# Layer 1's k placed by transfers inside SBUF, and layer 1's normalisation moved from ScalarE to GpSimd

## The chip, the cores and the metric

One Trainium2 chip, one core of it. The metric is the device time of one execution in microseconds (us); the kernel before was run three times: 1116.78, 1117.99 and 1119.48 us, median 1117.99 us.

## What is computed

The input is 8 sequences of 512 tokens with 128 channels. There are two layers. In each, the input is normalised over its channels, and the sum of an attention-like part and a feed-forward part is added to it.

```python
xn = _layernorm(x)                       # layer 0
x = x + _L0_attn_ref(xn, ...) + _L0_ffn_ref(xn, ...)   # state-space scan; one of 8 experts per token
xn = _layernorm(x)                       # layer 1
x = x + _L1_attn_ref(xn, ...) + _L1_ffn_ref(xn, ...)   # windowed attention; gated feed-forward

# inside _L1_attn_ref
q = _split_heads(x @ Wq + bq)            # 16 heads of 8 channels
k = _split_heads(x @ Wk + bk)
v = _split_heads(x @ Wv + bv)
scores = jnp.einsum('bhqd,bhkd->bhqk', q, k) / math.sqrt(HEAD_DIM)
scores = scores + _sliding_window_mask(s, WINDOW_SIZE)   # 32 positions to either side
```

## The kernel before, in words

**Stages.** The work is a pipeline over the 8 sequences, written out by hand. A turn is one pass of `iterations` (line 460); it has 28 slots, and `plan()` (line 80) lists what is done in each slot. In turn `it`, four lanes run side by side: "pre" prepares the scan of sequence it+1 (projections, convolution, gates), "scan" does the 16 steps of the scan of sequence it, "attn" does layer 1 of sequence it-1, and "late" and "finish" end layer 1 of sequence it-2. Each engine walks through the same list of units in the same order and does its own part of each, so every engine is a queue in order, and only semaphores tie the queues together. The experts of layer 0 run beside the first turns.

**The scan.** In each step n, ScalarE makes the decays (`decays`, line 911: two exponentials, dA), VectorE multiplies the input by a broadcast row into PSUM (`times_b`, line 725: dBu), VectorE scans (line 733: hst), and hst times another broadcast row gives hc, on GpSimd (line 1100), or on VectorE in steps 2, 3 and 15 (lines 743, 749). TensorE sums hc into y_bank (`sum_y`, line 1189). The broadcast rows come by the SP queue (`bc_rows`, line 530) into a ring of 4 buffers, bcr; after step k's unit "spread" the rows of step k+3 are sent for, and that waits until hc of step k-1 is done.

**Layer 1's front, slots 0 to 6 of a turn.** Slot 1: x1r (line 831). Slot 2, unit ln_a: VectorE's statistics (lines 837 to 844), then GpSimd's power and product (lines 1124, 1126: rstd1, shift1). Slot 3: step 2 of the scan, then ln_b: ScalarE normalises four blocks of 128x128 into xn1 (line 968), TensorE transposes each (line 1250), ScalarE copies the bank to xn1T (line 971). The pre lane's conv1 (VectorE, line 761) and the matmul of zg0 (line 1202) stand behind it. Slot 4: q and k (TensorE line 1254), ScalarE writes q in four copies, each with its own scale, into qbd (line 976), and k into kT (line 985): kT has four row blocks, heads 4r to 4r+3 of k lie in partitions 32r to 32r+31 of block r, and the rest of kT is zero. In the same slot stand the pre lane's tanh (line 935, with a load of the function table ahead of it) and sg0 (VectorE line 772), which needs that tanh. Slot 5: step 3 of the scan, v0 and v1 (TensorE 1261, ScalarE 990), conv2, and the tanh for sg1. Slot 6: v2, v3, conv3, sg1. Slot 7: step 4 of the scan. The first scores, which read kT, stand in slot 10 (line 1273).

**What sets the order around the change.** On ScalarE: the decays of step 3, then xn1, the copy to xn1T, the table load, the tanh for sg0, four qbd, four kT, the decays of step 4, v0, v1, the tanh for sg1. On VectorE: scan 2, dBu 3, hc 2, conv1 (two instructions), sg0, scan 3, dBu 4, hc 3, four of conv, sg1, scan 4. On TensorE: sum_y of step 1, the four transposes, zg0, q, k. On GpSimd: hc 0 and hc 1 (slots 0, 1), line 1124 and line 1126, then nothing of the scan before hc 4 in slot 7; line 1114 (the product of the finish lane) stands in slot 5. On the SP queue: in slot 0 the 16 + 4 + 1 transfers of `own_heads` (line 535), then the rows of steps 4 and 5, then in slot 5 those of step 6, in slot 7 of step 7.

**Buffers.** rbuf (line 266) holds the routing's logits in the first turn and zeros for one transfer; after that it is unused.

Of the kernel before, what the change touches and what calls it, by code (L numbers as in the profile page):

```python
# [11 lines left out]
ALU = mybir.AluOpType  # L12
# [182 lines left out]
def program(nc, hidden, pack, wx_d, ffn_d, xn_d, xs_d, ys_d, bc_d, rd_d, out):  # L195
    ctx = ExitStack()
    with ctx:
# [134 lines left out]
        xgT = [p_flat[:, 3 * L + k * P:3 * L + (k + 1) * P] for k in range(MOE_BANKS)]  # L332
        h_T = [fh[:, k, :] for k in range(MOE_BANKS)]
        o_own = fth
        rd_rows = y_out[:].rearrange("p j d -> p (j d)")
        ys = [y_out[:], fsg[:].rearrange("p (j d) -> p j d", d=H)]

# [42 lines left out]
        s_slot = sem("slots_of_sequence")  # L380
        s_moe = sem("expert_rows_in")
        s_conv = sem("conv_steps")
        s_tap = sem("first_tap_ready")
        s_tg = sem("gate_tanh_ready")
        s_xsq = sem("xsq_ready")
# [93 lines left out]
        @block.sync  # L479
        def _(sp):  # L480
            def x_load(k):
                sp.dma_start(xa[k % 4], seq(hidden, k)).then_inc(s_xa[k % 4], 16)
            x_load(0)
            x_load(1)
            sp.dma_start(pk[:], pack).then_inc(s_pack, 16)
            x_load(2)
            x_load(3)
            sp.dma_start(ffn_i, ffn_d).then_inc(s_ffn, 16)

            def weights(m):  # L490
                e = sp.value_load(tile_e[0:1, m:m + 1], min_val=0, max_val=E - 1)
                sp.dma_start(wx[m % WX_RING], wx_d[:, bass.ds(e, 1), :].rearrange("p o c -> p (o c)")).then_inc(
                    s_wx[m % WX_RING], 16)

            def early(name, k):
                if name == "norm":
                    sp.wait_ge(s_axn, (k + 1) * NT)
                    sp.dma_start(seq(xn_d, k), xna[k]).then_inc(s_xast[k], 16)
                    if k + 4 < B:
                        x_load(k + 4)  # L500
                    if k == 0:
                        sp.wait_ge(s_xast[0], 16)
                        sp.dma_start(x_in[:], seq(xn_d, 0)).then_inc(s_xin, 16)
                elif name == "scatter":
                    sp.wait_ge(s_route, ROUTE_TILES)
                    for m in range(3):
                        weights(m)
                elif name == "gather":
                    sp.wait_ge(s_scat, 16 * TT)
                    for k in range(B):  # L510
                        sp.wait_ge(s_xast[k], 16)
                    for r in range(2):
                        sp.dma_start(xg[r], tiles(xs_d, r)).then_inc(s_xg[r], 16)
                    for m in range(3, WX_RING):
                        weights(m)
                elif name == "xt":
                    r = k // MG
                    if k % MG == MG - 1 and r + 2 < NM // MG:
                        sp.wait_ge(s_xgT, k + 1)
                        sp.dma_start(xg[r % 2], tiles(xs_d, r + 2)).then_inc(s_xg[r % 2], 16)  # L520
                elif name == "add":
                    r = k // MG
                    if k + WX_RING < NM or k % MG == MG - 1:
                        sp.wait_ge(s_myc, k + 1)
                    if k + WX_RING < NM:
                        weights(k + WX_RING)
                    if k % MG == MG - 1:
                        sp.dma_start(tiles(ys_d, r), ys[r % 2]).then_inc(s_yst[r % 2], 16)

            def bc_rows(b, n):  # L530
                before(sp, s_hc, b * N + n - RING + 1)
                rows = bc_d[b:b + 1].rearrange("o (k n) t -> o n k t", k=2)
                sp.dma_start(bcr[n % RING][:], rows[:, n, :, :].to_broadcast([P, 2, L])).then_inc(s_bcr[n % RING], 16)

            def own_heads(b):
                done1(sp, b, f"gate{HC - 1}")
                done1(sp, b, "oL")
                for r in range(RG):
                    for h in range(4):
                        q = slice(32 * r + HD * h, 32 * r + HD * h + HD)  # L540
                        sp.dma_start(o_own[q, :], o_all[q, h, :, :].rearrange("p g q -> p (g q)")).then_inc(s_own, 16)
                done1(sp, b, "rdT")
                for r in range(RG):
                    rows = rd_d[b, r] if isinstance(b, int) else rd_d[bass.ds(b, 1), r].rearrange("o h g q -> (o h) g q")
                    sp.dma_start(rows.rearrange("h g q -> g h q"), rdenT[r * G:(r + 1) * G, :, :]).then_inc(s_rdst, 16)
                sp.wait_ge(s_rdst, b * 64 + 64)
                before(sp, s_out, b * 16)
                rows = rd_d[b:b + 1] if isinstance(b, int) else rd_d[bass.ds(b, 1)]
                sp.dma_start(rd_rows, rows.rearrange("o r h g q -> (o r h) (g q)").unsqueeze(1).to_broadcast(
                    [RG * 4, HD, L])).then_inc(s_rdin, 16)  # L550

            def body(it, par):
                for name, k, b, odd in units(it):
                    early(name, k)
                    if name == "dtT":
                        done0(sp, b, "dtT")
                        sp.dma_start(bc_d[b], dtT[R:XW, :]).then_inc(s_bcd, 16)
                    if name == "start":
                        sp.wait_ge(s_bcd, b * 16 + 16)
                        for n in range(RING - 1):  # L560
                            bc_rows(b, n)
                    if name == "spread" and k + RING - 1 < N:
                        bc_rows(b, k + RING - 1)
                    if name == "spread" and k == 0 and b >= 2:
                        own_heads(b - 2)
                    if name == "xnT" and (not isinstance(b, int) or b + 1 < B):
                        full0(sp, b, "xnT")
                        sp.wait_ge(s_xast[b + 1], 16)
                        sp.dma_start(x_in[:], seq(xn_d, b + 1)).then_inc(s_xin, 16)
                    if name == "rdT":  # L570
                        if b >= B - 2:
                            own_heads(b)
                    if name == "y_out":
                        done1(sp, b, "fin")
                        sp.dma_start(seq(out, b), y_out[:]).then_inc(s_out, 16)
                    if name == "rows":
                        done1(sp, b - 1, "out")
                        sp.dma_start(x_res[:], seq(hidden, b)).then_inc(s_xres, 16)
            for name, k in LEAD:
                early(name, k)  # L580
            for it in range(-1, B + 2):
                body(it, it % 2)
            sp.wait_ge(s_out, 16 * B)
# [302 lines left out]
        def _(act):  # L886
# [76 lines left out]

            def layer1(name, k, b, par):
                if name == "ln_b":
                    act.wait_ge(s_rstd1, b * 2 + 2)
                    for j in range(NT):
                        s.activation(xn1[:, j, :], x1r[par][:, j, :], ACT.Identity, bias=shift1[:, j:j + 1],
                                     scale=rstd1[:, j:j + 1]).then_inc(s_xn1, 1)
                    full1(act, b, "xnT")  # L970
                    s.copy(xn1T[:, WIN:WIN + L], w1k("xnT")[:]).then_inc(free1("xnT"), 1)
                elif name == "q":
# [5 lines left out]
                    last.then_inc(free1(name), 1)  # L978
                elif name == "k":
                    full1(act, b, name)  # L980
                    if isinstance(b, int) and b == 0:
                        act.wait_ge(s_clear, 1)
                    for r in range(RG):
                        q = slice(32 * r, 32 * r + 32)
                        last = s.activation(kT[q, r, WIN:WIN + L], w1k(name)[q, :], ACT.Identity, bias=pc("bk")[q, :])
                    last.then_inc(free1(name), 1)
                elif name in ("v0", "v1", "v2", "v3"):
                    j = int(name[1:])
                    full1(act, b, name)
# [54 lines left out]
        def _(pool):  # L1044
# [58 lines left out]
            def body(it, par):  # L1103
                for name, k, b, odd in units(it):
# [14 lines left out]
                    elif name == "bc":  # L1119
                        bc(b)  # L1120
                    elif name == "ln_a":
                        pool.wait_ge(s_stat1, b * 10 + 10)
                        before(pool, s_xn1, b * NT)
                        g_.tensor_tensor(rstd1[:], var1[:], minus_half[:, 0:NT], ALU.pow).then_inc(s_rstd1, 1)
                        pool.wait_ge(s_rstd1, b * 2 + 1)
                        g_.tensor_tensor(shift1[:], shift1[:], rstd1[:], ALU.mult).then_inc(s_rstd1, 1)
            iterations(pool, body)


        @block.tensor  # L1130
        def _(pe):
# [100 lines left out]
            def layer1(name, k, b, par):  # L1232
# [31 lines left out]
                elif name == "scores":  # L1264
                    key = f"s{k}"
                    if k == 0:
                        done1(pe, b, "q")
                        done1(pe, b, "k")
                    take1(pe, b, key)
                    v = 0 if k == 0 else (2 if k == G - 1 else 1)  # L1270
                    t.matmul(w1k(key)[:, 0:RG * KW], identb[:], bandb[:, v, :, :].rearrange("p r k -> p (r k)"),
# [118 lines left out]
```

## Time and profile before

| what | value |
|---|---|
| runs | 1116.78, 1117.99, 1119.48 us; median 1117.99 |
| profiled execution, its own time | 1115.84 us |
| its span | 1114.1 us |
| granted TensorE clock, mean | 0.925 of full speed |
| TensorE matmul busy | 861.4 us, 77% |
| VectorE busy | 810.0 us, 73% |
| ScalarE busy | 679.8 us, 61% |
| GpSimd busy | 386.2 us, 35% |

The span runs from the first to the last instruction of the program; the execution's own time has 1.7 us more around it. Busy shares are means over the whole span. The times of the rows below are microseconds from the start of this span.

### The profile page before, as it was taken

The page shows a single profiled execution, that of the slowest core. Times are in us where ns is not written, and L with a number is a line of the kernel's source. Part 1 is how long each engine was busy: PE and PEld are TensorE (multiplying, and loading weights), DVE is VectorE, ACT ScalarE, POOL GpSimd, SP SyncE. Part 2 cuts the span into 40 slices and gives each one's busy share as a digit, 9 for nine tenths or more (in the row PEclk, how much of TensorE's full clock was granted, in tenths as well). Part 3 has the DMA queues.
Part 4 walks back from the last instruction along what each step waited for, and adds up shares of the span by engine and source line. Part 5 has one row for each costly group of instructions (what it writes and reads, how often), then busy time and mean ns, then how long its engine had stood idle before and what let it go on. Part 6 is the DMA issues. An engine that isn't in the chain of part 4 may idle for free.

```text
span 1114.1 us, 13822 instructions
## 1 busy us (share of the span) xinstructions
PE 861.4 (77%) x4346; PEld 477.5 (43%) x4346; DVE 810.0 (73%) x1010; ACT 679.8 (61%) x2045; POOL 386.2 (35%) x228
## 2 busy tenths in 40 slices
PE   3553879886697779777977797788878886897893
PEld 2412667663343444334434443343335333443532
DVE  7764444677978897889788968897889788974120
ACT  2132556665577657766776667666756684685680
POOL 3175122213632263226322632254225422641000
PEclk9556999998999999999998989999989899999995
DMA  8164779963331433244324332443234333430001
GB/s 295 39 212 120 228 230 287 264 192 76 82 97 58 123 86 97 57 119 91 97 59 115 93 85 70 105 102 89 71 93 102 80 77 105 102 88 11 19 1 30
DMA packets 85304, 121.14 MB, mean 109 GB/s; under 512 B 8560, under 2 KB 43760, under 8 KB 85104
## 3 DMA queue, kind: packets, MB, share of 16 engines
q1 hardware_dynamic: 78944, 113.45, 36.6%
q0 software_dynamic: 6288, 6.82, 2.7%
q8 instruction: 35, 0.57, 0.2%
q14 instruction: 37, 0.30, 0.1%
HBM read 105.82 MB, written 12.32 MB: 106 GB/s over the span
## 4 chain that ended last, share of the span: by engine, by line
PE 37%; DVE 26%; issue 11%; POOL 11%; ACT 10%; DMA 3%; SPq 1%; DVEq 0%; POOLq 0%; ACTq 0%
PE y_bank L1189 11%; DVE hst L733 10%; POOL hc L1100 4%; PE more L1287 4%; DVE dBu L725 4%; POOL xs_d L1068 3%; POOL x_res L1084 3%; PE work_l L1273 2%; PE work L1273 2%; ACT qbd L976 2%; PE work L1202 2%; ACT dA L917 2%; DVE dc L810 2%; DVE nmax L847 1%; DMA hst<-in_hidden 1%
## 5 line engine op out<-in xcount | busy, mean ns | idle before, releaser
L1100 POOL TENSOR_TENSOR hc<-hst,bcr 128x1024 f32<-128x1024 f32 x102 | 244.3, 2395 | 530.6 <-DVE dBu L725 488.0
L1189 PE MATMUL y_bank<-hc,pk 128*128 128x512 f32 x512 | 269.8, 653 | 83.1 <-POOL hc L1100 66.0
L733 DVE TENSOR_TENSOR_SCAN hst<-dA,dBu 128x1024 f32<-128x1024 f32 x128 | 291.5, 2278 | 3.4 <-issue 2.9
L725 DVE TENSOR_TENSOR dBu<-dtu,bcr 128x1024 f32<-128x1024 f32 x128 | 175.7, 1373 | 12.9 <-DVE hst L733 0.5
L917 ACT ACTIVATE dA<-dt,neg_a 128x511 f32<-128x511 f32 x256 | 171.6, 726 | 17.7 <-DVE hst L733 14.4
L1189 PEld LDWEIGHTS y_bank<-hc,pk 128*128 128x128 f32 x512 | 94.7, 201 | 186.2 <-POOL hc L1100 81.5
L1011 ACT COPY pT<-more 96x512 f32<-96x512 f32 x128 | 74.4, 581 | 100.0 <-PE more L1287 98.3
L1287 PE MATMUL more<-pk,pexp 128*96 128x128 f32 x512 | 102.6, 291 | 10.9 <-ACT pexp L1001 10.4
L1287 PEld LDWEIGHTS more<-pk,pexp 128*96 128x96 f32 x512 | 61.3, 128 | 84.7 <-issue 58.6
L1001 ACT ACTIVATE pexp<-work,nmax 128x96 f32<-128x96 f32 x256 | 83.2, 338 | 15.9 <-DVE nmax L847 15.8
L1001 ACT ACTIVATE pexp<-work_l,nmax 128x96 f32<-128x96 f32 x256 | 83.1, 338 | 1.2 <-DVE nmax L847 1.2
L847 DVE TENSOR_REDUCE nmax<-work 128x4 f32<-128x384 f32 x64 | 35.4, 553 | 51.2 <-PE work L1228 47.7
L1084 POOL DMA_INDIRECT x_res<-ys_d,slot_b x32 | 51.2, 1601 | 9.0 <-issue 9.0
L1273 PE MATMUL work_l<-kT,qbd 128*128 128x384 f32 x128 | 53.2, 498 | 0.0
L1001 ACT ACTIVATION_READ_ACCUMULATOR pexp<-work_l,nmax 128x1 f32 x256 | 52.2, 204 | 0.0
L1001 ACT ACTIVATION_READ_ACCUMULATOR pexp<-work,nmax 128x1 f32 x256 | 51.9, 203 | 0.0
L1273 PE MATMUL work<-kT,qbd 128*128 128x384 f32 x128 | 51.7, 486 | 0.0
L847 DVE TENSOR_REDUCE nmax<-work_l 128x4 f32<-128x384 f32 x64 | 35.4, 553 | 21.7 <-PE work_l L1228 21.1
L1202 PE MATMUL work<-xnT,pk 128*128 128x512 f32 x64 | 38.6, 688 | 14.4 <-ACT hs L930 9.4
L1114 POOL TENSOR_TENSOR fth<-fth,y_out 128x512 f32<-128x512 f32 x8 | 11.6, 1445 | 109.5 <-DMA y_out<-rd_d 109.5
L928 ACT ACTIVATE z<-work,half_c 128x512 f32<-128x512 f32 x16 | 12.4, 777 | 51.5 <-PE work L1202 44.8
L864 DVE TENSOR_TENSOR y_out<-x1r,work 128x512 f32<-128x512 f32 x8 | 5.5, 682 | 40.8 <-PE work L1316 40.8
(303 smaller groups left out, 1475.7 us busy)
## 6 DMA issues: line engine op xcount, KB each, us to landing
bcr<-bc_d SPq DMA_DIRECT2D x128, 512.0 KB
qbd<-in_wx SPq DMA_DIRECT2D x8, 578.0 KB, 4.2
o_all<-in_wx SPq DMA_DIRECT2D x8, 578.0 KB
pT<-in_wx SPq DMA_DIRECT2D x8, 578.0 KB
kT<-in_wx SPq DMA_DIRECT2D x8, 578.0 KB, 5.1
vw<-in_wx SPq DMA_DIRECT2D x8, 578.0 KB, 5.2
xs_d<-rbuf POOLq DMA_DIRECT2D x1, 2560.0 KB, 9.8
hst<-in_hidden SPq DMA_DIRECT2D x8, 256.0 KB, 4.9
```

The source lines that it names most:

```text
L725: v.tensor_tensor(dBu[:], dtu[par], bcr[n % RING][:, 0:1, :].to_broadcast([P, NH, L]), ALU.mult).then_inc(s_dBu, 1)
L733: v.tensor_tensor_scan(hst[n % 2][:].rearrange("p h t -> p (h t)"), dA[n % 2][:].rearrange("p h t -> p (h t)"), dBu[:].rearrange("p h t -> ...
L847: v.tensor_reduce(nmax[:, k, :], w1k(f"s{k}")[:, 0:RG * KW].rearrange("p (r k) -> p r k", r=RG), AX_X, ALU.max, negate=True).then_inc(s_nm ...
L917: s.activation(dA[n % 2][:, h, 1:L], dt[par][:, h, 1:L], ACT.Exp, scale=neg_a[:, h, n:n + 1]).then_inc(s_dA, 1)
L1001: last = s.activation(pexp[k % 2][:, r, :], w1k(f"s{k}")[:, r * KW:(r + 1) * KW], ACT.Exp, bias=nmax[:, k, r:r + 1], accum_out=den[:, r, k ...
L1011: s.copy(pT[k % 4][:], w1k(f"pT{k}")[0:KW, :]).then_inc(free1(f"pT{k}"), 1)
L1084: g_.indirect_dma_start(x_res[:, j, :], None, ys_d.rearrange("i j p d -> (i j p) d"), bass.IndirectOffsetOnAxis(ap=slot_b[:, j:j + 1], axi ...
L1100: g_.tensor_tensor(hc[n % 2][:], hst[n % 2][:], bcr[n % RING][:, 1:2, :].to_broadcast([P, NH, L]), ALU.mult).then_inc(s_hc, 1)
L1189: last = t.matmul(y_bank[h][:], ident, hc[n % 2][:, h, :], start=False, stop=(n == N - 1))
L1202: t.matmul(bank0[:], pc("in_proj")[:, k * P:(k + 1) * P], xnT[:], start=True, stop=True).then_inc(s_full0, 1)
L1273: last = t.matmul(w1k(key)[:, 0:RG * KW], qbd[:, k, :, :].rearrange("p h q -> p (h q)"), kT[:, :, k * GQ:k * GQ + KW], start=False, stop=True)
L1287: last = t.transpose(w1k(key)[0:KW, r * P:(r + 1) * P], pexp[k % 2][:, r, :], ident)
```

## The change

ScalarE no longer normalises xn1: GpSimd does it, with four tensor_scalar instructions (times rstd1, plus shift1) behind its own power and product in slot 2. ScalarE writes k once, as one 128x512 tile with its bias, into the free half of rbuf (k_flat_b); the SP queue waits for that in slot 4, and then issues four transfers, each of 32 partitions x 512 f32, from k_flat_b into the four row blocks of kT. TensorE's first scores wait for these transfers (semaphore s_kin) in place of ScalarE's write. ScalarE's next write of k waits for the transfers of the sequence before.

```diff
+        k_flat_b = rbuf[:, 1, :]
...
+        s_kin = sem("k_blocks_in")
...
 (SP queue, body)
+                    if name == "k":
+                        if b == 0:
+                            sp.wait_ge(s_clear, 1)
+                        done1(sp, b, "k")
+                        for r in range(RG):
+                            q = slice(32 * r, 32 * r + 32)
+                            sp.dma_start(kT[q, r, WIN:WIN + L], k_flat_b[q, :]).then_inc(s_kin, 16)
...
 (ScalarE, layer1)
                 if name == "ln_b":
-                    act.wait_ge(s_rstd1, b * 2 + 2)
-                    for j in range(NT):
-                        s.activation(xn1[:, j, :], x1r[par][:, j, :], ACT.Identity, bias=shift1[:, j:j + 1],
-                                     scale=rstd1[:, j:j + 1]).then_inc(s_xn1, 1)
                     full1(act, b, "xnT")
                     s.copy(xn1T[:, WIN:WIN + L], w1k("xnT")[:]).then_inc(free1("xnT"), 1)
...
                 elif name == "k":
                     full1(act, b, name)
-                    if isinstance(b, int) and b == 0:
-                        act.wait_ge(s_clear, 1)
-                    for r in range(RG):
-                        q = slice(32 * r, 32 * r + 32)
-                        last = s.activation(kT[q, r, WIN:WIN + L], w1k(name)[q, :], ACT.Identity, bias=pc("bk")[q, :])
-                    last.then_inc(free1(name), 1)
+                    before(act, s_kin, b * 64)
+                    s.activation(k_flat_b, w1k(name)[:], ACT.Identity, bias=pc("bk")).then_inc(free1(name), 1)
...
 (GpSimd, ln_a)
                         g_.tensor_tensor(shift1[:], shift1[:], rstd1[:], ALU.mult).then_inc(s_rstd1, 1)
+                        pool.wait_ge(s_rstd1, b * 2 + 2)
+                        for j in range(NT):
+                            g_.tensor_scalar(xn1[:, j, :], x1r[(par + odd) % 2][:, j, :], rstd1[:, j:j + 1], shift1[:, j:j + 1],
+                                             ALU.mult, ALU.add).then_inc(s_xn1, 1)
...
 (TensorE, scores, k == 0)
-                        done1(pe, b, "k")
+                        pe.wait_ge(s_kin, b * 64 + 64)
```

## Rows read from the trace of the kernel before

**Rows 1.** The page: the chain that ended last, shares of the span by engine.

```profile
PE 37%; DVE 26%; issue 11%; POOL 11%; ACT 10%; DMA 3%; SPq 1%; DVEq 0%; POOLq 0%; ACTq 0%
```

**Rows 2.** Waits: who waited for whom; total us, times, longest.

```profile
DVE sg L772 <- ACT tg L935: 17.4, 11, 3.9
```

**Rows 3.** Timeline, turn from 478 us: start, us, engine, line, operation, [idle before].

```profile
485.43 0.20 POOL L1126 TENSOR_TENSOR shift<-shift,rstd 128x4 f32<-128x4 f32 x1
485.68 1.88 PE L1189 MATMUL y_bank<-hc,pk 128*128 128x512 f32 x4
486.53 1.23 DVE L725 TENSOR_TENSOR dBu<-dtu,bcr 128x1024 f32<-128x1024 f32 x1
488.26 1.64 ACT L968 ACTIVATE xn<-x1r,shift,rstd 128x128 f32<-128x128 f32 x4
488.81 1.41 DVE L761 SCALAR_TENSOR_TENSOR z<-hs,half_c,z 128x512 f32<-128x512 f32 x2
488.89 1.39 PE L1250 MATMUL work_l<-pk,xn 128*128 128x128 f32 x4 [1.33 <-ACT xn L968]
489.06 9.52 SPq L533 DMA_DIRECT2D bcr<-bc_d  x4
490.32 0.58 ACT L971 COPY xn1T<-work_l 128x512 f32<-128x512 f32 x1 [0.42 <-PE work_l L1250]
492.84 0.69 DVE L772 SCALAR_TENSOR_TENSOR sg<-tg,work 128x512 f32<-128x512 f32 x1 [2.62 <-ACT tg L935]
495.35 2.74 ACT L985 ACTIVATE kT<-work_l,pk 32x512 f32<-32x512 f32 x4
501.07 0.69 DVE L772 SCALAR_TENSOR_TENSOR sg<-tg,work 128x512 f32<-128x512 f32 x1 [0.23 <-ACT tg L935]
508.18 1.23 DVE L725 TENSOR_TENSOR dBu<-dtu,bcr 128x1024 f32<-128x1024 f32 x1
```

**Rows 4.** The same view, turns from 588 us (sg0, sg1) and 814 us (sg0).

```profile
604.46 0.69 DVE L772 SCALAR_TENSOR_TENSOR sg<-tg,work 128x512 f32<-128x512 f32 x1 [3.94 <-ACT tg L935]
...
613.12 0.69 DVE L772 SCALAR_TENSOR_TENSOR sg<-tg,work 128x512 f32<-128x512 f32 x1 [0.66 <-ACT tg L935]
...
829.75 0.69 DVE L772 SCALAR_TENSOR_TENSOR sg<-tg,work 128x512 f32<-128x512 f32 x1 [2.93 <-ACT tg L935]
```

**Rows 5.** The same view: the turns from 925 us and 1018 us, and the first.

```profile
936.23 1.65 ACT L968 ACTIVATE xn<-x1r,shift,rstd 128x128 f32<-128x128 f32 x4 [3.93 <-POOL shift L1126]
...
947.01 2.29 DVE L733 TENSOR_TENSOR_SCAN hst<-dA,dBu 128x1024 f32<-128x1024 f32 x1 [2.90 <-issue]
...
1035.74 1.11 PE L1261 MATMUL work_l<-pk,xn1T 128*96 128x128 f32 x8 [1.50 <-ACT kT L985]
...
270.05 0.68 DVE L772 SCALAR_TENSOR_TENSOR sg<-tg,work 128x512 f32<-128x512 f32 x1
```

**Rows 6.** Groups of GpSimd by line and shape: busy us, mean ns.

```profile
L1124 POOL TENSOR_TENSOR rstd<-var,minus_half 128x4 f32<-128x4 f32 x8 | 8.3, 1039 | 14.3 <-DVE shift L844 14.3
```

**Rows 7.** Timeline at 526 us and 938 us: GpSimd and VectorE side by side.

```profile
526.08 2.93 POOL L1100 TENSOR_TENSOR hc<-hst,bcr 128x1024 f32<-128x1024 f32 x1
526.76 4.17 DVE L725 TENSOR_TENSOR dBu<-dtu,bcr 128x1024 f32<-128x1024 f32 x1
528.39 1.45 POOL L1093 TENSOR_TENSOR xdn<-xdr,pk 128x384 f32<-128x384 f32 x1
531.01 2.35 POOL L1100 TENSOR_TENSOR hc<-hst,bcr 128x1024 f32<-128x1024 f32 x1 [1.18 <-DVE dBu L725]
...
938.23 1.22 DVE L743 TENSOR_TENSOR hc<-hst,bcr 128x1024 f32<-128x1024 f32 x1
938.23 2.34 POOL L1114 TENSOR_TENSOR fth<-fth,y_out 128x512 f32<-128x512 f32 x1 [2.04 <-DMA y_out<-rd_d]
```

**Rows 8.** Timeline: the product on GpSimd at 491 us, and the SP queue's issues.

```profile
474.79 10.68 SPq L541 DMA_DIRECT2D fth<-o_all  x16
...
491.86 1.27 POOL L1114 TENSOR_TENSOR fth<-fth,y_out 128x512 f32<-128x512 f32 x1 [6.22 <-DMA y_out<-rd_d]
512.69 0.81 PE L1273 MATMUL work<-kT,qbd 128*128 128x384 f32 x2
```

## The prediction

> **What bounds the kernel now.** I read the chain that ended last, then the waits, then the timeline of each turn's first 25 us. The chain has no single owner: TensorE 37%, VectorE 26%, ScalarE 10%, GpSimd 11% [rows 1]. So a change is worth what it does at the wait that ends last where it is made, and the place is layer 1's front. There VectorE, which carries the scan, stands still for ScalarE: sg0 and sg1 wait for a tanh, 17.4 us in 11 waits [rows 2]. In the turn from 478 us sg0 waits 2.62 us and sg1 0.23 us [rows 3]. Three turns have this form (from 366, 478 and 703 us). Two have the form of 588 us, with 3.94 and 0.66 us [rows 4]; the other, from 814 us, has 2.93 [rows 4] and 0.67. ScalarE reaches that tanh late because it first does four xn1 blocks (488.26 to 489.90), waits for the transposes, copies at 490.32 and loads a table; sg0 starts 2.52 us after the copy starts [rows 3]. The last turn with a scan has no tanh, but VectorE waits 2.90 us before scan 4, whose decays stand behind kT on ScalarE [rows 5]. The turn after it has no scan: TensorE waits 1.50 us for the bank that kT is read from [rows 5]. In the first such turn sg0 does not wait [rows 5]; there VectorE itself is the bound.
>
> **xn1 leaves ScalarE.** ScalarE loses 1.64 us a turn [rows 3]. The gain is less, since the transposes become the limit: TensorE's sum_y ends at 485.68 + 1.88 = 487.56, the transposes start at 488.89 now [rows 3]. They can come 1.33 us earlier if GpSimd is in time, and copy, table load, tanh and sg0 come with them. I take 1.33 in all five turns with a wait at sg0; the other four repeat these rows.
>
> **xn1 on GpSimd.** No GpSimd tensor_scalar is in the trace. From below: its smallest product, 4 elements a partition, takes 0.20 us [rows 3]. From above: the power on 4 elements, 1.04 us [rows 6]. Nearest are the products: 2.35 us for 1024 elements [rows 7] and 1.27 for 512 [rows 8], so 2.11 ns an element and 0.19 us fixed, and 0.46 us for 128. I take 0.45 each, 1.8 us for four, from 485.63 (end of line 1126) to 487.43. The fourth transpose now starts at about 489.9 and would at 488.6: in time. GpSimd has nothing of the scan there before step 4. Behind the new work stands only line 1114, which starts at 491.86 [rows 8].
>
> The two engines hold each other up. At 526 us VectorE's dBu (1.23 us elsewhere) took 4.17 us, until two products of GpSimd had ended; at 938 us GpSimd's product took 2.34 instead of 1.27 us beside VectorE's hc [rows 7]. Whoever is in first keeps the other out. Here GpSimd is in at 485.63, while VectorE scans, and scans are not slowed in the trace; dBu 3 is due at 486.53 [rows 3]. It would wait until 487.43, 0.90 us. VectorE had 2.62 us to spare at sg0: its conv1 ends at 488.81 + 1.41 = 490.22, then at 491.12, and the tanh allows sg0 at 492.84 - 1.33 = 491.51. So the delay is covered, with 0.39 us left. In general, with t for one block, sg0 gains the smaller of 1.33 and W - (4t - 0.90), W being its wait: 3.52 - 4t for the three turns, 4.84 - 4t and 3.83 - 4t for the two.
>
> The Trainium skill (SBUF — State Buffer, "Who interferes with whom") says the same of the pair of ports, and that the first to issue holds it for one whole instruction. The trace agrees as far as the 4.17 us go, but there a second GpSimd instruction still kept VectorE out. Taken strictly, the rule lets VectorE in between two blocks; that is the second rival below.
>
> The Trainium skill (GPSIMD Engine Reference, "Engine selection") puts one-input work on GpSimd at roughly line rate, against about twice VectorE's time with two inputs. No run here shows it; an estimate by it is some 0.3 us a block, and the sum would be 1 us better.
>
> **k written once.** Four instructions take 2.74 us on ScalarE [rows 3]; one of the same length takes a quarter, so 2.05 us go. Where sg1 waits, only its wait is won, since VectorE's own eight us of work between sg0 and sg1 then bound: 0.23 in three turns, 0.66 and 0.67 in two. In the turn from 925 us the decays come 2.05 earlier, inside VectorE's 2.90. In the last, TensorE's 1.50.
>
> **The transfers.** Sixteen issues of this kind take 10.68 us on the SP queue [rows 8], so four take 2.7. k is written at about 494.5 (now 495.35 to 498.09, less 1.33 and 2.05, with the q copies unchanged), issued by 497.3, and read by the scores at 512.69 [rows 8], 511 then. I cost the landing at nothing: 13 us cover it; gone, it would cost its length once a turn. Behind SP's wait stand the scan rows of steps 6 and 7. Those of step 6 go out with the four from 489.06 now, at about 497.5 then; they are used at 508.18 [rows 3], 506.5 then. 9 us cover them. Step 7's wait for hc 3 anyway. The ring's slots, and rbuf, are free.
>
> **Where it doesn't help.** In the turns from 925 and 1018 us xn1 already waited for GpSimd [rows 5], so the move costs 4 x 0.45 - 1.65 = 0.15 each. In the first turn VectorE has nothing to spare and loses the 0.90. Later stages of a turn hang on VectorE's u and scans, so I let the gain pass through.
>
> **Sum:** 5 x 1.33 = 6.65; sg1 3 x 0.23 + 0.66 + 0.67 = 2.02; 2.05 - 0.15 = 1.9; 1.5 - 0.15 = 1.35; minus 0.9. That is 11.0 us. The profiled execution has 1115.84, so 1104.8; the median is 2.15 above it, so **1107**. At t = 0.20 it is 6.65 + 2.02 + 2.05 + 1.5 = 12.2, so 1105.8. At t = 1.04: 3 x (-0.64) + 0.68 - 0.33 + 2.02, then 2.05 - 2.51, 1.5 - 2.51 and -3.26, together -4.3, so 1122.3. It turns at about t = 0.93.
>
> **Rivals.**
> 1. *Only k pays.* The transposes come no earlier than now (GpSimd's blocks are slower beside VectorE, or t is about 0.8), but nothing is lost: 2.02 + 1.9 + 1.35 - 0.9 = 4.4 us, so 1113.6. For it: 2.34 instead of 1.27 us [rows 7].
> 2. *VectorE gets in between, slower than before.* dBu 3, hc 2 and conv1 follow one another, each with two SBUF inputs. If dBu 3 enters at 486.53 and GpSimd's last two blocks wait for all three, they end at 490.22 + 0.90 = 491.12, the copy starts 0.42 later at 491.54 instead of 490.32: 1.22 lost in three turns (-3.66), +0.10 and -0.91 in the two with longer waits, 2.02 from sg1, in the turn from 925 us (hc 2 ends 939.45 [rows 7], xn1 at 940.35 instead of 937.88) 2.05 - 2.47, then 1.35 without a scan, and 1.22 + 2.62 = 3.84 lost in the first. Together -5.4, so 1123.4. It decides from the moment that two blocks have to wait. Against it: at 526 us back-to-back GpSimd work was not interrupted [rows 7]. The page named above speaks for it.
> 3. *t near 1 us:* 1122, as worked out. Against it: the power is the dearest row.
> 4. *Nothing arrives at the end:* the stages after slot 10 hang on TensorE and GpSimd, which hold 48% of the chain [rows 1], and take the gain back: 1117 to 1118. Against it: their first work of the turn waits for VectorE.
>
> **Chances.** My forecast 0.60; rival 1, 0.14; rival 2, 0.11; rival 3, 0.05; rival 4, 0.10. Under 0.2% (2.2 us) a measurement of this kernel can't tell from no change; most of rival 4 falls there. Faster 0.76, same 0.08, slower 0.16. The likeliest case's own range is 1105 to 1110; the range 1102 to 1116 takes in rival 1, the scatter of the runs and some gain I haven't seen; it leaves out rivals 2 and 3 and most of 4.
>
> **What would show it.** GpSimd's line of xn1 at about 450 ns; dBu 3 at some 2.1 us; the wait at sg0 down to about 0.4 us and at sg1 gone; ScalarE's busy time down by 8 x (1.64 + 2.05) = 29.5 us; no wait on s_kin at the first scores; SP's rows of step 6 eight us later and no VectorE wait for them. Wrong if xn1 on GpSimd ends after 489 us in the turn of rows 3, if dBu 3 runs between blocks, or if a VectorE wait of like size shows up later in each turn.

## The result, and the profile after

The changed kernel takes 1121.45 us (median of 12 runs, 1119.51 to 1123.58), the kernel before 1118.16 (median of 12). The ratio is 1.0029, with a 95% interval of 1.0019 to 1.0039: slower by 0.3%, where the prediction had 1107 us and a range that ended at 1116. The profiled execution took 1120.89 us, its span 1119.0. Ratios here and below are estimates from the executions that were not disturbed, against those of the kernel before beside them, and not quotients of the medians; one of the 12 of experiment 1, with 1134.53 us at a granted clock of 0.814, is left out of its ratio.

The page of the changed kernel, busy times and the chain that ended last, to be read against [rows 1]:

```profile
PE 861.7 (77%) x4346; PEld 479.2 (43%) x4346; DVE 807.5 (72%) x1010; ACT 651.4 (58%) x1989; POOL 419.7 (38%) x260
PE 35%; DVE 29%; POOL 13%; issue 12%; ACT 4%; DMA 4%; SPq 1%; DVEq 0%; POOLq 0%; ACTq 0%
```

ScalarE has lost 28.4 us of work, and its share of the chain went from 10% to 4%. What it left, GpSimd and VectorE took up. GpSimd's new line, and the wait at sg0, which stood in [rows 2]:

```profile
L1130 POOL TENSOR_SCALAR xn<-x1r,rstd,shift x32: 447/452/2517, 266.7 to 1033.4; 128x128 f32<-128x128 f32 x32
DVE sg L781 <- ACT tg L944: 19.4, 7, 3.3
```

Of the 32 blocks the shortest took 447 ns, the median 452, the longest 2517. The length of a block alone is what the prediction took, 0.45 us. But the wait at sg0 and sg1 is 19.4 us in 7 waits, and was 17.4 in 11. The timeline of one turn shows why (this is the turn of [rows 3]; start, us, engine, line; the blocks one by one):

```profile
489.01 2.27 DVE L742 TENSOR_TENSOR_SCAN hst<-dA,dBu 128x1024 f32<-128x1024 f32 x1
490.60 0.45 POOL L1130 TENSOR_SCALAR xn<-x1r,rstd,shift 128x128 f32<-128x128 f32 x1
491.04 0.45 POOL L1130 TENSOR_SCALAR xn<-x1r,rstd,shift 128x128 f32<-128x128 f32 x1
491.38 1.23 DVE L734 TENSOR_TENSOR dBu<-dtu,bcr 128x1024 f32<-128x1024 f32 x1
491.47 2.52 POOL L1130 TENSOR_SCALAR xn<-x1r,rstd,shift 128x128 f32<-128x128 f32 x1
492.53 1.22 DVE L752 TENSOR_TENSOR hc<-hst,bcr 128x1024 f32<-128x1024 f32 x1
493.66 1.53 DVE L770 SCALAR_TENSOR_TENSOR z<-hs,half_c,z 128x512 f32<-128x512 f32 x2
493.97 1.38 POOL L1130 TENSOR_SCALAR xn<-x1r,rstd,shift 128x128 f32<-128x128 f32 x1
495.77 0.59 ACT L976 COPY xn1T<-work_l 128x512 f32<-128x512 f32 x1 [2.56 <-PE work_l L1255]
498.30 0.69 DVE L781 SCALAR_TENSOR_TENSOR sg<-tg,work 128x512 f32<-128x512 f32 x1 [3.11 <-ACT tg L944]
506.82 2.28 DVE L742 TENSOR_TENSOR_SCAN hst<-dA,dBu 128x1024 f32<-128x1024 f32 x1
```

The first two blocks run under scan 2 and take 0.45 us each. VectorE's dBu starts at 491.38, nine hundredths before the third block, and keeps its 1.23 us. The third block takes 2.52: it ends at 493.99, 0.24 us after hc, so it waited for dBu and hc. It was let in ahead of conv1, whose first instruction takes 0.11 us more than its second:

```profile
493.66 0.86 DVE L770 SCALAR_TENSOR_TENSOR z<-hs,half_c,z 128x512 f32<-128x512 f32 x1
494.44 0.75 DVE L770 SCALAR_TENSOR_TENSOR z<-hs,half_c,z 128x512 f32<-128x512 f32 x1
```

The fourth takes 1.38 and ends at 495.35, 0.16 us after the second of these and 0.83 after the first: it waited for both. The four blocks have these lengths, within 0.02 us, in all of turns 1 to 6. Turn 7 has no convolution; VectorE goes from hc to scan 3, and there the fourth block takes 0.45 beside it:

```profile
943.52 2.28 DVE L742 TENSOR_TENSOR_SCAN hst<-dA,dBu 128x1024 f32<-128x1024 f32 x1
943.83 0.45 POOL L1130 TENSOR_SCALAR xn<-x1r,rstd,shift 128x128 f32<-128x128 f32 x1
```

So dBu, hc and conv1, which read two tiles of SBUF each, shut a block out, and the scan, which takes its dBu from PSUM, does not: the first two blocks and turn 7's fourth run beside one. In turns 1 to 6 the four blocks take 4.75 us in place of 1.8. In this turn ScalarE stands idle for 2.56 us before its copy, and VectorE waits 3.11 us at sg0 for what it has itself held up.

The same in numbers for every turn: from the start of scan 2 to the start of scan 4 (line 733 before, 742 after), each the difference of two starts in the traces.

| turn | before | changed | k part alone | xn1 part alone | both, VectorE held |
|---|---|---|---|---|---|
| 1 | 14.59 | 17.77 | 14.49 | 19.32 | 15.48 |
| 2 | 17.53 | 17.81 | 17.20 | 18.13 | 15.48 |
| 3 | 17.52 | 17.81 | 17.21 | 19.00 | 16.67 |
| 4 | 19.28 | 17.81 | 17.20 | 18.99 | 16.03 |
| 5 | 17.51 | 17.96 | 18.76 | 19.00 | 15.47 |
| 6 | 19.29 | 17.81 | 17.21 | 18.99 | 16.54 |
| 7 | 12.30 | 13.31 | 10.12 | 15.50 | 11.37 |

Turns 2, 3 and 5 are the three of the prediction, 4 and 6 the two with a longer wait, 7 the last with a scan. Changed less before: +3.2 in turn 1, +0.3, +0.3 and +0.45 in the three, -1.5 twice, +1.0 in turn 7, together 2.3 us. One scan later, turn 7 has lost 1.4 more (18.64 us from scan 2 to scan 5 in place of 16.19). After the last copy to xn1T (1027.47 before, 1034.46 changed), in the turn without a scan, the changed kernel needs 84.5 us in place of 86.6: 2.0 less, where 1.5 was predicted. The k part alone needs 84.5 there too. Of the span's 4.9 us another 1.1 are there before turn 1's scan 1 (252.32 against 251.26), ahead of the first use of the change; the rest is spread over the later parts of turns.

### The profile page after: what moved, and what is told of

It is laid out like the page before. It is cut to its first block, busy times and chain, and to the rows that moved or that the text cites. A ratio compares the mean times of both kernels' runs of the same rounds, so it can differ in the third digit from the quotient of the medians.

```text
span 1119.0 us, 13837 instructions
## 1 busy us (share of the span) xinstructions
PE 861.7 (77%) x4346; PEld 479.2 (43%) x4346; DVE 807.5 (72%) x1010; ACT 651.4 (58%) x1989; POOL 419.7 (38%) x260
## 4 chain that ended last, share of the span: by engine, by line
PE 35%; DVE 29%; POOL 13%; issue 12%; ACT 4%; DMA 4%; SPq 1%; DVEq 0%; POOLq 0%; ACTq 0%
DVE hst L742 11%; PE y_bank L1194 10%; PE more L1292 4%; POOL hc L1101 3%; POOL xs_d L1069 3%; POOL x_res L1085 3%; POOL xn L1130 3%; DVE dBu L734 3%; PE work_l L1278 2%; PE work L1278 2%; DVE dc L819 2%; DMA hst<-in_hidden 1%; PE work L1213 1%; DVE z L770 1%; DVE nmax L856 1%
## 5 line engine op out<-in xcount | busy, mean ns | idle before, releaser
L1207 PE MATMUL work<-xnT,pk 128*128 128x512 f32 x64 | 41.0, 729 | 11.8 <-ACT hs L939 9.4
L1130 POOL TENSOR_SCALAR xn<-x1r,rstd,shift 128x128 f32<-128x128 f32 x32 | 34.1, 1075 | 0.9
```

What stands on the lines that cost most here:

```text
L1130: g_.tensor_scalar(xn1[:, j, :], x1r[(par + odd) % 2][:, j, :], rstd1[:, j:j + 1], shift1[:, j:j + 1], ALU.mult, ALU.add).then_inc(s_xn1, 1)
```

## The experiments

Eleven kernels. The theory (A): the k part pays as predicted, and xn1 on GpSimd is spoiled by VectorE's instructions with two SBUF inputs getting between the blocks. Its rivals: the transfers cost the time (B), or GpSimd is slow for a reason of its own (C).

**1. The k part alone.** The GpSimd loop is taken out and ScalarE's is put back. The first lines are `layer1` of ScalarE, the others GpSimd's.

```diff
                 if name == "ln_b":
+                    act.wait_ge(s_rstd1, b * 2 + 2)
+                    for j in range(NT):
+                        s.activation(xn1[:, j, :], x1r[par][:, j, :], ACT.Identity, bias=shift1[:, j:j + 1],
+                                     scale=rstd1[:, j:j + 1]).then_inc(s_xn1, 1)
                     full1(act, b, "xnT")
...
                         g_.tensor_tensor(shift1[:], shift1[:], rstd1[:], ALU.mult).then_inc(s_rstd1, 1)
-                        pool.wait_ge(s_rstd1, b * 2 + 2)
-                        for j in range(NT):
-                            g_.tensor_scalar(xn1[:, j, :], x1r[(par + odd) % 2][:, j, :], rstd1[:, j:j + 1], shift1[:, j:j + 1],
-                                             ALU.mult, ALU.add).then_inc(s_xn1, 1)
```

> Only the k part of the change: xn1 stays on ScalarE as before, k is written once and placed by four transfers. Theory A (what slows the changed kernel is xn1 on GpSimd, whose blocks are shut out by VectorE's two-input work; the k part pays as predicted): in the turns where sg1 waits, its 0.23 (three) or 0.66 us (two) is won, 2.05 in the last turn with a scan, 1.5 in the one after: 5.6 us, ratio near 0.995, 1112 to 1114. Theory B (the transfers or SP's wait cost time, and xn1 is harmless): as slow as the changed kernel, 1.003 or more.

Measured: 1114.12 us, ratio 0.9949 (0.9927 to 0.9971). That is 5.7 us by the ratio, 3.2 to 8.2 by its interval; 5.6 were expected. The turns bear it out where the clock is the same: some 0.3 us less in turns 2 and 3 (0.23 predicted), 2.2 in turn 7 (2.05), 2.0 behind the last copy (1.5). The SP queue of this kernel and the end of the sg1 wait, in the third turn:

```profile
496.43 2.44 SPq L581 DMA_DIRECT2D kT<-rbuf  x4
498.92 1.12 SPq L535 DMA_DIRECT2D bcr<-bc_d  x2
501.10 0.68 DVE L781 SCALAR_TENSOR_TENSOR sg<-tg,work 128x512 f32<-128x512 f32 x1
```

Four transfers are issued in 2.44 us and the rows of steps 6 and 7 follow at 498.92; sg1 waits no longer. No engine waits for kT in the list of waits. Theory B falls.

**2. The xn1 part alone.** The kernel before, with ScalarE's loop taken out and GpSimd's put in.

> Only the xn1 part: the four blocks on GpSimd, k written by ScalarE in four as before. Theory A: as the changed kernel, and without the k gain some 4 to 6 us slower than it: ratio 1.007 to 1.009, 1126 to 1128; four blocks take about 4.8 us in the turns with a convolution. Theory B: 1.00 or below.

Measured: 1127.48 us, ratio 1.009 (1.0076 to 1.0105). All of the loss is here, 10 us. With the k part's 5.7 it leaves 4.4, and the changed kernel has 3.3: the two parts add up within the intervals. In the trace the blocks take 4.75 us in turns 1 to 6, as expected and as in the changed kernel.

**3. Both parts, VectorE held.** One wait: VectorE starts the dBu of step 3 only when the four blocks are done.

```diff
                 if n + 1 < N:
+                    if n == 2 and b >= 1:
+                        dve.wait_ge(s_xn1, b * NT)
                     times_b(n + 1, b, par)
```

> The changed kernel with one wait more: VectorE issues the dBu of step 3 only when GpSimd's four xn1 blocks of that turn are done, so nothing of VectorE with two SBUF inputs can shut them out. Theory A: the blocks take 1.8 us together, sg0 comes 1.3 us earlier than in the kernel before, and the sum of the prediction comes true: 1105 to 1109. A rival C (GpSimd is slow there for another reason, its issue or its semaphores): the blocks still take 4 us or more, VectorE now waits for them too, and the time is above the changed kernel's 1121.

Measured: 1105.11 us, ratio 0.9878 (0.9864 to 0.9893). One added wait makes the changed kernel 1.5% faster (0.9878 against 1.0029, some 16 us). Its timeline in turn 4:

```profile
596.23 2.27 DVE L742 TENSOR_TENSOR_SCAN hst<-dA,dBu 128x1024 f32<-128x1024 f32 x1
597.83 1.74 POOL L1132 TENSOR_SCALAR xn<-x1r,rstd,shift 128x128 f32<-128x128 f32 x4
599.60 1.23 DVE L734 TENSOR_TENSOR dBu<-dtu,bcr 128x1024 f32<-128x1024 f32 x1 [1.10 <-POOL xn L1132]
603.21 0.68 DVE L783 SCALAR_TENSOR_TENSOR sg<-tg,work 128x512 f32<-128x512 f32 x1
606.73 1.23 DVE L734 TENSOR_TENSOR dBu<-dtu,bcr 128x1024 f32<-128x1024 f32 x1 [0.65 <-DMA bcr<-bc_d]
```

The four blocks take 1.74 us, VectorE waits 1.10 for them, and the wait at sg0 is gone. Theory C falls. The last row is a new wait: the dBu of step 4 now waits 0.65 us for its broadcast rows, which stand on the SP queue behind `own_heads`. Its SP rows in that turn:

```profile
586.86 10.70 SPq L543 DMA_DIRECT2D fth<-o_all  x16
597.61 1.84 SPq L547 DMA_DIRECT2D rd_d<-rdenT  x4
600.51 0.59 SPq L551 DMA_DIRECT2D y_out<-rd_d  x1
601.48 0.90 SPq L535 DMA_DIRECT2D bcr<-bc_d  x2
```

Issued at 601.48, landed by 606.7: within 5.2 us. Two of the seven turns have such a wait, 2.0 us together, so it is the next limit in some turns and not in all.

**4. The xn1 part alone, VectorE held.** The wait of experiment 3 in the kernel of experiment 2.

> The xn1 part alone (k written in four by ScalarE, as before), with VectorE held until the four blocks are done. Theory A (the move of xn1 is worth what the prediction said, once nothing gets in between): five turns win some 1.3 us at sg0, the first loses about 0.9, the last two 0.15 each; 5 to 6 us below the kernel before, ratio 0.995. With the k part's 5 us it should add up to the 12 to 13 us of the version with both. Rival D (the two parts only help together): ratio 0.999 or more.

Measured: 1110.62 us, ratio 0.9931 (0.9916 to 0.9947), 7.7 us; 5 to 6 were expected. 7.7 and 5.7 make 13.4, and the version with both has 13.6, each known to some 2 us. Rival D falls.

**5. VectorE held one instruction later.** dBu goes ahead; the hc of step 2 waits for the blocks.

```diff
                     before(dve, s_hc, b * N + n)
                     before(dve, s_ys, b * (N + 1) + n)
+                    if n == 2 and b >= 1:
+                        dve.wait_ge(s_xn1, b * NT)
                     v.tensor_tensor(hc[n % 2][:], hst[n % 2][:], bcr[n % RING][:, 1:2, :].to_broadcast([P, NH, L]),
```

> The changed kernel with the wait for the four blocks one instruction later on VectorE: the dBu of step 3 goes ahead, the hc of step 2 waits. Theory A with a lock per instruction: the third block waits for that dBu alone (1.2 us) in place of dBu and hc (2.5 us), the fourth follows at once; the blocks end about 4.5 us after the start of scan 2, in place of 6.3 (changed) and 3.4 (held ahead of dBu); time between the two, 1108 to 1113.

Measured: 1106.22 us, ratio 0.9897 (0.9879 to 0.9914). In turn 4:

```profile
595.88 2.75 POOL L1132 TENSOR_SCALAR xn<-x1r,rstd,shift 128x128 f32<-128x128 f32 x4
596.66 1.23 DVE L734 TENSOR_TENSOR dBu<-dtu,bcr 128x1024 f32<-128x1024 f32 x1
598.77 1.23 DVE L754 TENSOR_TENSOR hc<-hst,bcr 128x1024 f32<-128x1024 f32 x1 [0.87 <-POOL xn L1132]
```

The blocks take 2.75 us, one more than when nothing is between them: the third waits for dBu alone and the fourth follows at once. They end at 598.63, 4.35 us after the start of scan 2 at 594.28, where 4.5 was expected. The time came out below the expected 1108 to 1113, and can't be told from experiment 3. By the traces VectorE waits less here for the blocks (0.87 in place of 1.10), and 1.9 us in six waits for a tanh (0.6 of it ahead of turn 1), where experiment 3 has none.

**6. Memsets in place of the blocks.** This leaves out the normalisation of layer 1 (xn1 is a constant); the waits and all other work stay.

```diff
-                            g_.tensor_scalar(xn1[:, j, :], x1r[(par + odd) % 2][:, j, :], rstd1[:, j:j + 1], shift1[:, j:j + 1],
-                                             ALU.mult, ALU.add).then_inc(s_xn1, 1)
+                            g_.memset(xn1[:, j, :], 0.5).then_inc(s_xn1, 1)
```

> The changed kernel with the four GpSimd tensor_scalars replaced by four memsets of the same size: the normalisation is left out, xn1 is a constant, all waits and all other work stay. If what shuts the blocks out is a read interface that both engines share, memsets, which read nothing, run through beside VectorE's dBu and hc: four in about 0.8 to 1 us, and the time falls to that of the held version or below it, 1100 to 1105. If any GpSimd work is shut out, the third memset takes some 2.3 us, as the third block does, and the time stays near 1120.

Measured: 1101.89 us, ratio 0.9854 (0.9834 to 0.9873). The four memsets and VectorE's next instruction, turn 4:

```profile
596.60 0.64 POOL L1130 MEMSET xn<- 128x128 f32 x4
597.43 1.24 DVE L734 TENSOR_TENSOR dBu<-dtu,bcr 128x1024 f32<-128x1024 f32 x1
```

They take 0.64 us, less than the 0.8 to 1 expected, and are through at 597.24, before dBu starts at 597.43. So the time fits the theory (no shut-out, no delay of VectorE), but the question of the run, whether an instruction that only writes is shut out, was not put: the two never met.

**7. Two blocks on GpSimd, two on ScalarE.** Blocks 0 and 1 end before dBu begins; a second semaphore, `s_xn1a`, counts ScalarE's, and all that waited for `s_xn1` waits for both (those lines are left out here). ScalarE's lines come first.

```diff
                 if name == "ln_b":
+                    act.wait_ge(s_rstd1, b * 2 + 2)
+                    for j in range(2, NT):
+                        s.activation(xn1[:, j, :], x1r[par][:, j, :], ACT.Identity, bias=shift1[:, j:j + 1],
+                                     scale=rstd1[:, j:j + 1]).then_inc(s_xn1a, 1)
...
                         pool.wait_ge(s_rstd1, b * 2 + 2)
-                        for j in range(NT):
+                        for j in range(2):
                             g_.tensor_scalar(xn1[:, j, :], x1r[(par + odd) % 2][:, j, :], rstd1[:, j:j + 1], shift1[:, j:j + 1],
                                              ALU.mult, ALU.add).then_inc(s_xn1, 1)
```

> The changed kernel with blocks 0 and 1 on GpSimd (done before the dBu of step 3 begins) and blocks 2 and 3 on ScalarE. Theory A: the copy to xn1T comes some 0.8 us earlier than in the kernel before, in the five turns that wait there, and the k part pays in full: 9 us below the kernel before, 1107 to 1111; better than the k part alone.

Measured: 1110.61 us, ratio 0.9933 (0.9916 to 0.995). ScalarE's share comes late because the decays of step 3 stand ahead of it. Turn 4:

```profile
598.88 0.88 POOL L1137 TENSOR_SCALAR xn<-x1r,rstd,shift 128x128 f32<-128x128 f32 x2
601.38 0.87 ACT L979 ACTIVATE xn<-x1r,shift,rstd 128x128 f32<-128x128 f32 x2
605.20 0.69 DVE L782 SCALAR_TENSOR_TENSOR sg<-tg,work 128x512 f32<-128x512 f32 x1 [1.86 <-ACT tg L946]
```

sg0 still waits, 1.86 us. The time is within the expected 1107 to 1111, 7.5 us below the kernel before; of that the k part has 5.7, so this half of the xn1 part gives some 1.8 us, where the whole of it gives 7.9 in experiment 3. That it is better than the k part alone is not shown by the times, whose intervals overlap; the stretches of the table in turns 2, 3, 4 and 6, 16.4 us in place of 17.2, do show the expected 0.8.

**8. The blocks on VectorE.** Behind scan 2, ahead of dBu 3; GpSimd keeps the power and the product of the statistics and loses the loop; the last sequence's blocks are normalised in VectorE's own `ln_b`.

```diff
+            def normalise(b):
+                dve.wait_ge(s_rstd1, b * 2 + 2)
+                for j in range(NT):
+                    v.tensor_scalar(xn1[:, j, :], x1r[b % 2][:, j, :], rstd1[:, j:j + 1], shift1[:, j:j + 1],
+                                    ALU.mult, ALU.add).then_inc(s_xn1, 1)
...
+                if n == 2 and b >= 1:
+                    normalise(b - 1)
                 if n + 1 < N:
                     times_b(n + 1, b, par)
```

> The changed kernel with the four xn1 blocks on VectorE, behind scan 2 and ahead of the dBu of step 3; GpSimd keeps the power and the product. Theory A: VectorE has 2.6 us to spare at sg0 and the blocks take it some 0.8 us; no engine shuts another out: 1104 to 1109, at least as good as the version in which VectorE waits. Rival C: no better than the k part alone (1112 to 1114), since sg0 then waits for VectorE itself.

Measured: 1103.59 us, ratio 0.9883 (0.9861 to 0.9904). Turn 4:

```profile
595.80 1.09 DVE L740 TENSOR_SCALAR xn<-x1r,rstd,shift 128x128 f32<-128x128 f32 x4
596.80 1.23 DVE L734 TENSOR_TENSOR dBu<-dtu,bcr 128x1024 f32<-128x1024 f32 x1
600.40 0.68 DVE L789 SCALAR_TENSOR_TENSOR sg<-tg,work 128x512 f32<-128x512 f32 x1
```

VectorE needs 1.09 us for the four, about as much as it waits in experiment 3. The two versions can't be told apart by their intervals; both are some 1.2% faster than the kernel before and 1.5% faster than the changed one.

**9. Blocks 0 and 1 on GpSimd, 2 and 3 on VectorE.** Experiment 8 with `range(2, NT)` in `normalise` and a loop of two on GpSimd.

> Blocks 0 and 1 on GpSimd while VectorE is in scan 2, blocks 2 and 3 on VectorE behind scan 2, the k part as in the changed kernel: nothing is shut out and VectorE has two blocks less than in the version with all four on it. If the rest holds, 0.3 to 0.5 us a turn below that version's 1103.6: 1100 to 1104; if the gain there is not VectorE's own length, no difference (1103 to 1105).

Measured: 1105.4 us, ratio 0.9897 (0.9878 to 0.9916). The intervals overlap, so no gain over experiment 8 can be told; one of 2 us can't be excluded either. The trace shows five waits of a dBu for its broadcast rows, 2.6 us together, in place of two with 0.8 in experiment 8: what VectorE saves goes in part into that.

**10 and 11. One more GpSimd instruction ahead of the blocks.** [Rows 7] showed a dBu that waited through two GpSimd products; in the changed kernel dBu got in at a change of instruction. These two runs ask which it is when VectorE comes while GpSimd is busy. Run 10 adds one tensor_scalar over all 512 elements:

```diff
                         pool.wait_ge(s_rstd1, b * 2 + 2)
+                        g_.tensor_scalar(rbuf[:, 0, :], x1r[(par + odd) % 2][:].rearrange("p j d -> p (j d)"), rstd1[:, 0:1],
+                                         shift1[:, 0:1], ALU.mult, ALU.add)
                         for j in range(NT):
```

and in run 11 a product:

```diff
                         pool.wait_ge(s_rstd1, b * 2 + 2)
+                        g_.tensor_tensor(rbuf[:, 0, :], x1r[(par + odd) % 2][:].rearrange("p j d -> p (j d)"),
+                                         x1r[(par + odd) % 2][:].rearrange("p j d -> p (j d)"), ALU.mult)
                         for j in range(NT):
```

> The changed kernel with one more GpSimd tensor_scalar of 128x512 ahead of the four blocks (its result is not used). It begins where the first block did and is still running when VectorE's dBu of step 3 comes to wait. In the kernel before, two long GpSimd products in a row kept a waiting dBu out until both had ended. If a waiting dBu enters at the first change of instruction, the extra one (some 1.1 us) ends, then dBu and hc run, and the four blocks are shut out: they end 7 us or more after the start of scan 2. If GpSimd keeps the ports while it has the next instruction ready, the four blocks follow the long one at once (end about 4.1 us after the start of scan 2) and dBu takes 3 us or more in place of 1.23.

> As the run before, but the extra GpSimd instruction is a product with two inputs of 128x512 (1.27 us elsewhere), so that it is still running when the dBu of step 3 comes to wait, and the first block is ready to follow it. If the waiting dBu enters at the change of instruction: dBu shows about 0.5 us more than 1.23, and the blocks end at 7 us or more after the start of scan 2. If GpSimd keeps the ports while its next instruction is ready, as at 526 us in the kernel before: dBu shows 3 us or more and the four blocks end at about 4.7 us.

Run 10: 1129.8 us. Run 11: 1125.8 us (one execution each, so without an interval; the kernel before 1118.2 and 1118.8 beside them). In run 10 the long instruction took 0.77 us, not the 1.1 expected, and was over just before dBu came, turn 3:

```profile
494.36 0.77 POOL L1129 TENSOR_SCALAR rbuf<-x1r,rstd,shift 128x512 f32<-128x512 f32 x1
495.11 4.77 POOL L1132 TENSOR_SCALAR xn<-x1r,rstd,shift 128x128 f32<-128x128 f32 x4
495.15 1.23 DVE L734 TENSOR_TENSOR dBu<-dtu,bcr 128x1024 f32<-128x1024 f32 x1
```

The blocks are shut out again, the first of them now, though the profile has it start 0.04 us before dBu; the blocks end 7.12 us after the start of scan 2. So the question was not put: VectorE did not come while the long one ran. In run 11, turn 4, the product was still running when dBu came:

```profile
606.21 1.04 POOL L1129 TENSOR_TENSOR rbuf<-x1r 128x512 f32<-128x512 f32 x1
607.02 1.32 DVE L734 TENSOR_TENSOR dBu<-dtu,bcr 128x1024 f32<-128x1024 f32 x1
607.24 3.83 POOL L1132 TENSOR_SCALAR xn<-x1r,rstd,shift 128x128 f32<-128x128 f32 x2
```

dBu comes 0.23 us before the product's end (607.25), takes 1.32 us in place of 1.23 and gets in ahead of the first block, which by the profile started 0.01 us before that end. It is the same in all seven turns of this run, and in turns 1 to 6 the blocks end 7.28 us after the start of scan 2, where 7 or more was expected. The product took 1.04 us and not 1.27, and of the 0.23 us before its end only 0.09 shows in dBu, where 0.5 was expected. So a VectorE that has come shortly before the end of GpSimd's instruction does get in at the change. The difference to 526 us in the kernel before stays open: there the second product was on the engine 0.62 us before the first ended (528.39 against 526.08 + 2.93 = 529.01), and that may be what decides; no run separates it from the kind of the second instruction, a product there and a tensor_scalar here.

## Why the prediction was wrong

**The step that failed** is the paragraph on GpSimd holding the ports: "It would wait until 487.43, 0.90 us". It read from one kind of place [rows 7] that VectorE is kept out over a row of GpSimd instructions; the trace has that same pair of products six times (dBu 3.72 us once and 4.15 to 4.17 five times), which is no second kind of evidence. Its own times had dBu due at 486.53, just at the end of the second block (485.63 + 0.90), so the order hung on hundredths of a microsecond. The changed kernel shows the reverse: dBu keeps its 1.23 us and the third and fourth blocks take 2.52 and 1.38. Experiment 3, which makes the assumed order true by a wait, takes 1105.11 us, within 2 us of the forecast 1107; experiment 4 shows the same for xn1 alone. So the sum was near for a kernel in which the blocks are not interrupted, and this is not that kernel.

**Rival 2 was the case**, at a chance of 0.11 where it deserved more: VectorE got in between two blocks, as experiments 3, 5 and 11 confirm. The Trainium skill (SBUF — State Buffer, "Who interferes with whom") lets whoever issues first have the shared ports for one whole instruction. The trace agrees in that VectorE came in between two blocks. It does not agree as to who is next: the third block started at 491.47 and hc at 492.53, and yet the block ended behind hc. It was let in ahead of conv1, and the fourth was not let in between conv1's two instructions. What decides this stays open. Rival 2's size was off: 1123.4 against 1121.45. It let both last blocks run behind all of conv1 and had them end 6.97 us after the start of scan 2 (491.12 - 484.15), 0.90 us behind conv1. They end at 6.34, since the third was already through and the fourth, long begun, ends 0.16 us behind conv1.

**xn1 on GpSimd, 0.45 us a block:** right, 0.452 in the median; the prediction's other estimate, some 0.3, was too low. Rival 3 falls.

**1.33 us at sg0:** too small for the uninterrupted case. In experiment 3 sg0 starts 6.98 us after scan 2, and 8.69 before (492.84 - 484.15): 1.71. The term mis-sized is the transposes' 1.39 us [rows 3], which I kept as their length. Those were four transposes that each waited for a block of ScalarE. With the blocks ready they take less, as the rows of experiment 3 for TensorE and ScalarE in turn 4 show:

```profile
599.48 0.60 PE L1257 MATMUL work_l<-pk,xn 128*128 128x128 f32 x4
600.34 0.58 ACT L978 COPY xn1T<-work_l 128x512 f32<-128x512 f32 x1
```

They take 0.60 us, and the copy starts 4.11 us after scan 2 (600.34 - 596.23), where it was 6.17 (490.32 - 484.15) and I had 4.84. sg0 gains less than the copy, since with the held blocks VectorE comes to it later by itself: no wait stands before it in experiment 3's timeline. Five turns by 0.38 us are 1.9, near the 2 us by which experiment 3 beats the forecast, but in part by luck: the 1.9 us of the last turn with a scan came as 1.2 (15.03 us from scan 2 to scan 5 in place of 16.19). There hc 2 met the finish lane's product and took 2.28 us in place of 1.22:

```profile
931.12 1.83 POOL L1117 TENSOR_TENSOR fth<-fth,y_out 128x512 f32<-128x512 f32 x1 [0.55 <-DMA y_out<-rd_d]
931.75 2.28 DVE L754 TENSOR_TENSOR hc<-hst,bcr 128x1024 f32<-128x1024 f32 x1
```

**k written once, 5.6 us:** right; 5.7 measured (3.2 to 8.2). Four transfers in 2.44 us (2.7 said), no engine waits for them, and the rows of steps 6 and 7 behind them are in time.

**The first turn's loss of 0.90:** right for the uninterrupted case (14.59 to 15.48 in the table); in the changed kernel it is 3.2, the largest loss of all turns, since there nothing had been waiting.

**ScalarE 29.5 us less:** 28.4. The wait at sg0 "down to about 0.4 us" is 3.11 in this turn and 3.3 at most, the sign named beforehand for the forecast being wrong: xn1 ended 6.34 us after scan 2's start, 490.49 in the times of [rows 3] and so after 489, and dBu ran between blocks.

**Rival 1** came out at nearly its number (1113.6 against experiment 1's 1114.1), by chance: that sum has losses of the xn1 part in it, and experiment 1 is a kernel without that part.

**The turning point** of the prediction's sum is t = 0.91 and not 0.93: from -4.3 at 1.04 the sum rises by 32 us for each us of t. Nothing hangs on it.

## What to carry to other kernels

A row of short GpSimd instructions beside VectorE work with two SBUF inputs costs the length of VectorE's row, not of its own: here 1.8 us of blocks took 4.75. Before moving work to GpSimd, look at what VectorE has in the queue for the time it runs; if VectorE has slack there, make it wait for GpSimd, or give it the work: one wait turned +0.3% into -1.2%. And where one kind of collision in a trace is the only evidence of who wins, hold both orders as likely and price both.

## What the runs showed of the hardware that was not expected

**GpSimd's tensor_scalar** took 0.45 us for 128 elements a partition and 0.77 for 512: 0.83 ns an element and 0.34 us fixed (0.32 / 384, and 0.45 - 0.11). The products of [rows 7] and [rows 8] have 2.11 ns an element, 1.27 us for 512; run 11's product of x1r with itself took 1.04. One tensor_scalar over 512 elements took 0.77 us and the four over 128 took 1.74, but the four have a scale and a shift of their own each and can't be made one.

**The granted clock sets turns apart.** The two turns of 19.3 us in the kernel before had a mean granted clock of 0.88 from scan 2 to scan 4, those of 17.5 had 1.00, which is 2.4 GHz. In the k part alone it is turn 5 that had 0.88, with 18.76 us in place of 17.2. The columns are span, busy times, then granted clock, share of DMA and GB/s; the stretch is turn 4's front in the kernel before, then in the changed one:

```profile
592.00:606.00 14.00, 11.21 (x20) 4.01 (x19) 9.84 (x20) 8.99 (x15) 4.85 (x4) 0.76 0.50 124
```

```profile
599.00:613.00 14.00, 10.21 (x28) 4.27 (x27) 10.67 (x20) 8.20 (x13) 9.61 (x8) 1.00 0.37 103
```

A mean of 0.76 says that the clock was at its lower level, 1.2 GHz, for part of the stretch. The copy behind the transposes came 1.3 us later there after scan 2 (7.48 against 6.17), and the front was 1.8 us longer. That is what goes together; no run changed the clock alone. So part of the -1.5 us in turns 4 and 6 of the changed kernel may be the clock and not the change; it was not separated. The k part alone shows the same scatter between executions: three of its runs took 1106 to 1107 us at a mean clock of 0.926, eight took 1113 to 1117 at 0.912 to 0.920.
